# Three groups of transposes a step in place of five, in a macaron block of two top-2 expert layers around local attention

## The reference

```python
x = x + 0.5 * ffn(layernorm(x))     # 8 experts, the top 2 of a softmax, shares that sum to 1
x = x + attn(layernorm(x))          # 16 heads of 16; each row attends to rows s-1, s, s+1 (cyclic)
x = x + 0.5 * ffn(layernorm(x))     # the same weights as the first

# attn: xp = x @ Wp.T + bp; q, k, v = projections of xp; softmax over three scores; out @ Wo.T + bo
# ffn: gates = softmax(x @ Wg + bg); sum over the top 2 of share * (x @ We[e] + be[e])
```

## Time and profile before

| What | Value |
|---|---|
| median of three runs | 1111.66 us |
| the profiled execution | 1111.69 us, of which span 1109.8 us |
| busy PE / PEld | 1053.9 us (95%) / 882.1 us (79%) |
| busy DVE / POOL / ACT | 889.9 us (80%) / 719.9 us (65%) / 529.1 us (48%) |
| mean granted TensorE clock | 0.984 |

### The profile page before, as it was taken

The page is one execution under the profiler, slowest core; times in us unless marked ns, Lnnn a source line. Parts: engine busy times, 40 slices in busy tenths (PEclk is TensorE's granted clock), DMA queues, the critical chain, the costliest instruction groups (busy, mean ns, idle before and its releaser), DMA issues.

```text
span 1109.8 us, 17795 instructions
## 1 busy us (share of the span) xinstructions
PE 1053.9 (95%) x5459; PEld 882.1 (79%) x5459; DVE 889.9 (80%) x2441; ACT 529.1 (48%) x1181; POOL 719.9 (65%) x953
## 2 busy tenths in 40 slices
PE   5898799999999999999999999999999999999885
PEld 3677688888888888888888888888888888887663
DVE  3658688888889888888888888888888888888783
ACT  3254455454555554445554454455554545544331
POOL 2476476666777666677777666777766667665353
PEclk9899899999999999999999999999999999999998
DMA  5001000000000000000000000000000000000000
GB/s 166 10 30 36 12 15 6 19 20 21 19 20 20 11 10 20 20 20 20 21 20 1 20 20 20 20 20 20 16 6 20 20 20 20 11 10 1 20 10 19
DMA packets 12582, 23.04 MB, mean 21 GB/s; under 512 B 2212, under 2 KB 5812, under 8 KB 12488
## 3 DMA queue, kind: packets, MB, share of 16 engines
q1 hardware_dynamic: 9240, 13.37, 3.4%
q0 software_dynamic: 3248, 8.54, 2.8%
HBM read 12.47 MB, written 8.39 MB: 19 GB/s over the span
## 4 chain that ended last, share of the span: by engine, by line
PE 77%; DVE 6%; POOL 5%; issue 4%; SPq 3%; DMA 2%; ACT 2%; POOLq 0%; DVEq 0%; ACTq 0%
PE ffn_bank L887 17%; PE ffn_bank L888 17%; PE ffn_bank L889 17%; PE tr_bank L916 5%; PE tr_bank L928 4%; PE mix_bank L889 4%; PE mix_bank L888 4%; PE mix_bank L887 4%; SPq L250 2%; POOL base L331 2%; PE tr_bank L887 1%; PE tr_bank L888 1%; PE tr_bank L889 1%; DMA we_raw<-in_L_ffn_We 1%; POOL rstd L319 1%
## 5 line engine op out<-in xcount | busy, mean ns | idle before, releaser
L887 PE MATMUL ffn_bank<-we_hi,T_hi 128*128 128x512 f32 x1024 | 415.0, 405 | 3.5 <-DVE chain_sum L658 3.0
L889 PE MATMUL ffn_bank<-we_hi,T_lo 128*128 128x512 f32 x1024 | 403.1, 394 | 0.0
L888 PE MATMUL ffn_bank<-we_lo,T_hi 128*128 128x512 f32 x1024 | 401.8, 392 | 0.0
L453 ACT ACTIVATE we_raw<-ffn_bank,gate 128x256 f32<-128x256 f32 x512 | 208.6, 474 | 140.3 <-PE ffn_bank L889 138.8
L339 POOL TENSOR_TENSOR chain_sum<-chain_sum,we_raw 128x512 f32<-128x512 f32 x128 | 165.9, 1296 | 130.4 <-DVE chain_sum L658 129.1
L887 PEld LDWEIGHTS ffn_bank<-we_hi,T_hi 128*128 128x128 f32 x1024 | 194.3, 190 | 42.4 <-DVE chain_sum L658 4.6
L889 PEld LDWEIGHTS ffn_bank<-we_hi,T_lo 128*128 128x128 f32 x1024 | 193.7, 189 | 43.0
L888 PEld LDWEIGHTS ffn_bank<-we_lo,T_hi 128*128 128x128 f32 x1024 | 194.6, 190 | 34.5
L416 ACT CAST T_hi<-tr_bank 128x512 fp32r<-128x512 f32 x128 | 75.0, 588 | 168.1 <-PE tr_bank L916 167.9
L658 DVE SCALAR_TENSOR_TENSOR chain_sum<-ffn_bank,gate,chain_sum 128x256 f32<-128x256 f32 x256 | 111.7, 478 | 44.3 <-PE ffn_bank L889 43.6
L316 POOL TENSOR_TENSOR var_eps<-mean_var,eps 128x2 f32<-128x2 f32 x96 | 28.9, 301 | 136.9 <-DVE mean_var L576 136.9
(11 more groups left out here) (125 smaller groups left out, 1818.0 us busy)
## 6 DMA issues: line engine op xcount, KB each, us to landing
out_x<-y SPq DMA_DIRECT2D x31, 256.0 KB, 2.0
we_raw<-in_L_ffn_We SPq DMA_DIRECT2D x2, 1024.0 KB, 14.0
x_in<-in_L_attn_x,x_row POOLq DMA_INDIRECT x60, 3.1
x_in<-in_L_attn_x SPq DMA_DIRECT2D x2, 256.0 KB, 7.4
moved_qk<-qk SPq DMA_DIRECT2D x4, 124.0 KB
w_raw<-in_L_attn_Wq SPq DMA_DIRECT2D x1, 256.0 KB, 2.9
w_raw<-in_L_attn_Wk SPq DMA_DIRECT2D x1, 256.0 KB, 3.1
w_raw<-in_L_attn_Wv SPq DMA_DIRECT2D x1, 256.0 KB, 3.8
```

The lines of the kernel that those rows point to most:

```text
L453: last = nc.scalar.activation(scaled[:, f, t, half, j], ffn_bank[b][:, j * D:(j + 1) * D], ACT.Copy, scale=gate[:, 2 * f + t, e:e + 1])
L887: nc.tensor.matmul(dest, hi[:, t, k, :], w_hi_[:, k, c0:c1], start=(first and k == 0), stop=False, skip_group_check=not first)
L888: nc.tensor.matmul(dest, hi[:, t, k, :], w_lo_[:, k, c0:c1], start=False, stop=False, skip_group_check=not first)
L889: last = nc.tensor.matmul(dest, lo[:, t, k, :], w_hi_[:, k, c0:c1], start=False, stop=(k == KB - 1), skip_group_check=not first)
```

## The change

The transposes of a step stand in three groups: TA; TO with the gates' transpose, behind V; TD with TB, at the end. The projection moves behind the biases. The gates' transpose moves to columns 128 to 255 of `tr_bank[1]`, where it doesn't have to wait for `lo_step(TO)` (but for the drain's rounds). ACT and DVE take the high and low parts in the new order. On DVE `stats_step(LN1)` now stands ahead of `x2_step`. On POOL the order becomes `rstd_step(LN2)`, `rstd_step(LN1)`, `x1_bo_step`, `base_step(FFN2)`, `base_step(FFN1)`, `rstd_step(LN3)`. The drain (and for TD step 31) keeps the old order on PE, ACT and DVE, not on POOL. The diff, cut to its core:

```diff
@@ -172,7 +172,7 @@
         t_bank = {TO: tr_bank[0], TB: tr_bank[0], TA: tr_bank[1], TD: tr_bank[1]}
-        logit_bank, gateT_bank, proj_bank = tr_bank[1], tr_bank[0], tr_bank[1]
+        logit_bank, proj_bank = tr_bank[1], tr_bank[1]
@@ -220,6 +220,10 @@
+        def gateT_place(g):
+            return tr_bank[0][:, 0:PART] if g.const > PAIRS else tr_bank[1][:, PART:2 * PART]
@@ -367,16 +371,16 @@
                     rstd_step(LN2, s)
+                if (s + 2).within(PAIRS):
+                    rstd_step(LN1, s + 2)
+                if (s - 1).within(PAIRS + 1):
+                    x1_bo_step(s - 1)
...
                     base_step(FFN2, s - 4)
+                if (s + 1).within(PAIRS):
+                    base_step(FFN1, s + 1)
...
                     rstd_step(LN3, s - 3)
-                if (s - 1).within(PAIRS + 1):
-                    x1_bo_step(s - 1)
-                if (s + 2).within(PAIRS):
-                    rstd_step(LN1, s + 2)
-                if (s + 1).within(PAIRS):
-                    base_step(FFN1, s + 1)
@@ -425,7 +429,7 @@
                 await_(act, bias_done[FFN2], (g - 5).times(1))
-                nc.scalar.copy(gateT[:], gateT_bank[:, 0:PART]).then_inc(gateT_copied, 1)
+                nc.scalar.copy(gateT[:], gateT_place(g)).then_inc(gateT_copied, 1)
@@ -514,6 +518,7 @@
                 filling = s.reg is None and s.const < 4
+                drains, drained = s.const >= PAIRS - 1, s.const >= PAIRS
@@ -524,7 +529,7 @@
                     scale_step(FFN1, s, 1)
-                if (s - 3).within(GROUPS):
+                if (s - 3).within(GROUPS) and drained:
@@ -533,6 +538,8 @@
                     v_step(s - 1)
+                if (s - 3).within(GROUPS) and not drained:
+                    hi_step(TO, s - 3)
@@ -545,12 +552,14 @@
                     normalise_step(LN3, s - 3)
-                if (s - 3).within(GROUPS):
+                if (s - 3).within(GROUPS) and drains:
...
                     scale_step(FFN2, s - 4, 1)
+                if (s - 3).within(GROUPS) and not drains:
+                    hi_step(TD, s - 3)
@@ -816,17 +825,19 @@
                 gate_step(s + 1, gates_of(s), 0)
-                if (s - 3).within(GROUPS):
+                if (s - 3).within(GROUPS) and drained:
...
                 gate_step(s + 1, gates_of(s), 2)
+                if (s - 3).within(GROUPS) and not drained:
+                    lo_step(TO, s - 3)
...
                     stats_step(LN2, s)
+                if (s + 2).within(PAIRS):
+                    stats_step(LN1, s + 2)
...
                     stats_step(LN3, s - 3)
-                if (s + 2).within(PAIRS):
-                    stats_step(LN1, s + 2)
@@ -847,6 +858,8 @@
                     chain_step(FFN2, s - 4, 1, 3)
+                if (s - 3).within(GROUPS) and not drains:
+                    lo_step(TD, s - 3)
@@ -907,7 +920,7 @@
                     elif i == TB:
-                        pe.wait_ge(gateT_copied, (s + 1).times(1, 1))
+                        await_(pe, lo_done[TO], after_group(s - 3))
@@ -931,10 +944,10 @@
                 pe.wait_ge(gate_ops, (s + 1).times(GATE_OPS, GATE_OPS))
-                await_(pe, lo_done[TO], after_group(s - 3))
-                if s.reg is None:
+                if s.const >= PAIRS:
+                    await_(pe, lo_done[TO], after_group(s - 3))
                     await_(pe, lo_done[TB], after_pair(s - 1))
-                nc.tensor.transpose(gateT_bank[:, 0:PART], gate_parts[:].rearrange("p c k e -> p (c k e)"),
+                nc.tensor.transpose(gateT_place(s + 1), gate_parts[:].rearrange("p c k e -> p (c k e)"),
@@ -1016,6 +1029,7 @@
                 filling = s.reg is None and s.const < 4
+                drains = s.reg is None and s.const >= PAIRS - 1
@@ -1036,10 +1050,12 @@
                     ffn_step(FFN2, s - 4, s, 0, range(2, 3))
-                if (s - 3).within(GROUPS):
+                if (s - 3).within(GROUPS) and drained:
...
                     ffn_step(FFN1, s + 1, s + 1, 0, range(0, 2))
+                if (s - 3).within(GROUPS) and not drained:
+                    T_step(TO, s - 3, s)
@@ -1049,13 +1065,15 @@
                     bias_step(FFN1, s)
+                if (s - 3).within(GROUPS) and not drained:
+                    projection_step(s - 3, s)
...
                         ffn_step(FFN2, s - 4, s, 0, range(1, 4))
-                    ffn_step(FFN2, s - 4, s, 1, range(0, 2 if drained else 1))
+                    ffn_step(FFN2, s - 4, s, 1, range(0, 2 if drained else 1 if drains else 4))
...
                     T_step(TD, s - 3, s)
-                if (s - 4).within(GROUPS):
+                if (s - 4).within(GROUPS) and drains:
...
                     T_step(TB, s, s)

```

## The result

The changed kernel takes 1196.15 us, the median of six runs (1191.95 to 1197.38), against 1112.02 for the kernel before beside it: a ratio of 1.0751, 95% interval 1.0734 to 1.0769. The prediction was 1206, slower, within 1120 to 1240. The profiled execution has a span of 1195.5 us, 85.7 more than before.

The account below looks back on a forecast made before the run. PE was taken to bound the kernel, busy 827.90 of 829.10 us. 27 x (2.9 - 0.20) = 73, plus 18 for the clock and 3 for the ends, made 94; 1111.7 + 94 = 1206 us, range 1120 to 1240.

Parts of the forecast that it names:

- The order on POOL and the start of the score: POOL and DVE: three big additions in a row from 9.87 us behind the logits, score at 10.1, both falling together.
- the covered waits: V's copy, gates' copy and TO's low part on ACT and DVE: ready 0.3 to 0.4 us early, costed at nothing.
- The wait at bank 1: PE at the second tile's bank 1 waits for the chain's pair: 2.75 or 3.0 us a step, mean 2.9.
- turns: DVE's products and POOL's big additions alternate, one whole operation each; each addition among the products costs 1.0 to 1.15 us.
- The 0.24: DVE: the chain starts 0.24 us later than the end of the score's products.
- PE's own saving: PE's work and TD's wait together: 0.20 us less a step, 5.4 us in 27.
- TO's move: PE: 0.06 us saved at TO, 0.09 lost where Q starts without TO between, +0.03 a step.
- TD's wait: PE's wait for `normed` at TD goes: 0.17 us a step, 0.23 with the 0.06 at TD.
- the size of the groups: PE's transposes: joining groups brings nothing by itself; rival, a tail of 0.16 us per group, 1098 us, chance 0.02.
- The clock: TensorE at half clock for 3.4 us behind the wait, 1.7 us lost in 4 steps of 10: 18 us, bounds 0 and 46.
- The ends: Fill, step 31 and drain together: +3 us, bounds -3 and +7.
- LN3's lateness: Step 31, projection late but TD at its old place: LN3 ready some 1.5 us late.

Follow-up runs that it names:

- experiment 1: The changed kernel with only POOL's order put back to that of the kernel before: 1108.64 us, ratio 0.9966.
- experiment 6: Two kernels: the kernel before with only TD moved to TB's place, 1106.10 us; the changed kernel with POOL's old order and TD moved back, 1114.85 us.
- experiment 2: The changed kernel with `base_step(FFN1)` moved behind `rstd_step(LN3)` on POOL, so two additions meet the score's products: 1150.74 us, ratio 1.0344.
- experiment 5: The kernel before with nothing but POOL's new order: 1255.36 us, ratio 1.1281.
- experiment 3: The changed kernel with a fourth 128x512 addition on POOL behind `base_step(FFN1)` in steps 4 to 30: 1210.01 us, ratio 1.0874.
- experiment 4: The changed kernel with `stats_step(LN1)` put back behind `stats_step(LN3)` on DVE, POOL in its new order: 1226.78 us, ratio 1.1024.

## Why the prediction was right, point by point

**The order on POOL and the start of the score** were read right. Behind the logits (490.91 in the step shown) `x1_bo_step` began at 9.83, forecast 9.87; x2 at 8.32, forecast 8.34; the products at 10.06, forecast 10.1; they ended at 15.05, forecast 15.1. The biases came at 6.24 and the projection at 6.70, forecast 6.25 and 6.72, and none of the covered waits showed.

**The wait at bank 1** was forecast as 2.75 and 3.0 us, mean 2.9; PE's starts came 2.29 and 2.51 us late, mean 2.4. Order and turns were right: the products ended where they were forecast. The term that was too large is what lies behind the products. I put 0.24 between them and the chain, since the kernel before shows it; here the chain begins at 505.89, 0.07 before the merged row of products ends, so the pair ends at 15.85 where I had 16.2. The other 0.1 is what I put between the pair's end and PE's start; it is 0.05. The 0.24 was a poor row to read from: in its steps with six products the kernel before has 0.05, and experiment 1, whose products nobody holds up, has no gap either (the chain at 471.60, the products' end at 471.68). What makes the 0.24 wasn't tested.

The late start isn't the whole price. Against the 31.64 us of experiment 1 a step takes 2.47 and 2.69 more, mean 2.58: behind the late matmul the next one follows 0.34 us later, not 0.23, and the first matmul behind the eight transposes comes 0.06 later. I had 0.05 for all of that, inside the 2.9.

**PE's own saving** was forecast as 0.20 a step. Experiments 1 and 6 show 0.26 (31.90 to 31.64). TO's move was costed at +0.03; it costs nothing that shows. TD's wait went as forecast, and nothing came from the size of the groups.

So a step was to cost 2.9 - 0.20 = 2.7 more and cost 2.58 - 0.26 = 2.32. The sum had 27 of them, 73 us. Measured are 60.3 for 26 and 1.7 for the last (33.01 us against 31.32 from the logits of step 30 to those of 31), 62 together.

**The clock.** Four steps in ten at 1.7 us, 18 us, was a choice between bounds of 0 and 46. Ten of 26 steps were longer by 1.54: 15.4 us. The rows had one idle stretch each way, and both kinds do occur here. That the share came out so near is luck: in the experiments it lies between none (experiment 2) and 24 of 26 (experiment 5), and no row of before could tell which.

**The ends** were under-sized: +3, measured +9.9 - 1.7 = 8.2. The fill takes 4.9, 4.5 of it between the logits of steps 3 and 4 (37.17 us against 32.63), where one wait of PE for `normed` grew from 3.7 to 7.6 us and the clock stood at half for 3.4 us more; no row of before had decided it. Step 31 takes 1.3 more (forecast for LN3's lateness: 1.5). The drain takes 2.1 more in one step (25.99 against 23.87): 0.6 for the orders, as experiment 3 shows (24.45), and the rest is a stretch at half clock from 1109.2 on, where the kernel before has none.

The errors, 11 and 3 us too many and 5 too few, partly cancel: 94 forecast, 84 measured by the medians, 85.7 by the profiled executions. The mechanism stands on experiments 1, 2 and 3, which moved the number of additions among the products to none, two and four. One thing the prediction didn't say: had LN1's statistics stayed behind LN3's, the place of `base_step(FFN2)` would have cost more, without any turns (experiment 4).

## What to carry to other kernels

When a step moves on one engine, ask of each engine that runs in strict order what now stands ahead of the operation that PE waits for, and what runs beside it on the engine that takes turns with it. Here three 1.3 us additions of POOL, none of them late for anything, made PE wait 59.7 us in all since they fell among DVE's products. Count the possible turns, not the overlap: each of these additions that went ahead of a product delayed the rest by 1 us. And take a regrouping apart before it is judged: one of its four parts held all of the gain (0.5%), another all of the loss. LN1's statistics weren't moved by themselves.

## What the runs showed of the hardware

- The score's products on DVE (both inputs in SBUF) and POOL's big additions alternate, even where DVE's are issued back to back: three 128x512 products take 1.86 us, and 1.0 to 1.07 more for each addition, up to as many as there are gaps. The additions stretch as well, from 1.3 to 1.72 to 1.76 beside products of 512 and to about 1.5 beside those of 256. The rule of the Trainium skill, "SBUF — State Buffer", section "SBUF: two separate sides" (an exclusive lock for a whole instruction), agrees with these rows. What the rows add is that a queue of products doesn't keep the lock from one to the next.
- TensorE's clock after idle stretches of 2.12 to 2.35 us fell to half for 3.4 us in 10 of 26 steps, after stretches of 1.05 to 1.26 (experiment 2) in none; a fall cost 1.54 us of time. The length of the stretch alone doesn't decide: in experiment 4 the lower clock followed all 13 stretches of 2.77 us and none of the 13 of 3.37. What does decide stays open.
- Transposes of float32, 128x128, start 0.11 us apart, whether four or eight stand together (0.60 and 1.03 us), though each has a duration of 0.27.
